# Router and experts of block one: tokens on partitions, router and experts in one stage

## What is computed

```python
expert_scores = x_flat @ router_w.T                 # 1024 x 8
top_scores, selected = jax.lax.top_k(expert_scores, 2)
top_scores = softmax(top_scores)
x1 = ragged_dot(xb, w1b, gs)                        # bf16, 64 inner units of the token's expert
x3 = ragged_dot(xb, w3b, gs)
h = silu(x1) * x3
routed = ragged_dot(h, w2b, gs)
out = sum over the two experts of routed * score
```

## Time and profile before

| | us |
|---|---|
| median of 3 runs (lowest, highest) | 1874.4 (1871.81, 1875.39) |
| the profiled execution | 1873.63 |
| its span, first to last instruction | 1871.8 |
| TensorE busy (share of the span) | 1767.7 (94%) |
| VectorE busy | 1380.0 (74%) |
| ScalarE busy | 1099.3 (59%) |
| GpSimd busy | 529.7 (28%) |
| mean granted TensorE clock, share of full | 0.959 |

### The profile page before, as it was taken

How to read it: one execution, slowest core, us unless ns; L and a number is a source line. 1 busy time by engine, 2 the same in 40 slices (tenths; PEclk the granted TensorE clock), 3 DMA queues, 4 the chain that set the end, 5 groups by cost and what they waited for, 6 DMA issues and landing times. The chain is left out here.

```text
span 1871.8 us, 29442 instructions
## 1 busy us (share of the span) xinstructions
PE 1767.7 (94%) x10475; PEld 1065.4 (57%) x10476; DVE 1380.0 (74%) x1917; ACT 1099.3 (59%) x2196; POOL 529.7 (28%) x535
## 2 busy tenths in 40 slices
PE   6999999999999999899999959999999999789997
PEld 4433333333333333644444448888888888768885
DVE  4799999999999995455999666666656666556666
ACT  2488888888887877343888625444545454234342
POOL 7346333333444402022323321111211020022223
PEclk7799999999999999968999979999999999889998
DMA  7123322223222300102546210000000000043331
GB/s 167 23 49 62 56 43 43 53 47 68 66 44 60 67 18 10 35 17 43 115 96 157 68 36 16 16 22 14 22 9 22 14 11 0 10 118 105 112 118 54
DMA packets 50606, 98.62 MB, mean 53 GB/s; under 512 B 11545, under 2 KB 21881, under 8 KB 48971
## 3 DMA queue, kind: packets, MB, share of 16 engines
q1 hardware_dynamic: 50219, 96.83, 21.9%
q10 hardware_dynamic: 288, 0.49, 0.2%
HBM read 65.63 MB, written 15.92 MB: 44 GB/s over the span
## 5 line engine op out<-in xcount | busy, mean ns | idle before, releaser
L726 DVE TENSOR_REDUCE a_max_part<-psum 128x1 f32<-128x1024 f32 x640 | 753.7, 1219 | 86.9 <-PE psum L614 85.4
L797 ACT ACTIVATE a_probs<-psum 128x512 f32<-128x512 f32 x1280 | 671.7, 601 | 184.9 <-PE psum L665 184.3
L665 PE MATMUL psum<-a_q_max,a_k_rows 51*128 51x512 f32 x1280 | 462.1, 448 | 3.4 <-ACT a_probs L797 1.8
L665 PEld LDWEIGHTS psum<-a_q_max,a_k_rows 51*128 51x128 f32 x1280 | 212.1, 186 | 353.0 <-ACT a_probs L797 285.9
L614 PE MATMUL psum<-a_k_rows,a_q_rows 48*128 48x512 f32 x1280 | 356.8, 474 | 13.8 <-DVE a_max_part L726 4.6
L654 PE MATMUL psum<-a_probs,a_v_ext 128*32 128x512 f32 x2560 | 342.5, 607 | 0.0
L614 PEld LDWEIGHTS psum<-a_k_rows,a_q_rows 48*128 48x128 f32 x1280 | 154.5, 189 | 87.7 <-DVE a_max_part L726 69.6
L1915 PE MATMUL psum<-high_t_parts,high_gu 128*128 128x512 f32 x600 | 146.2, 394 | 6.8 <-DVE high_t_parts L2009 6.8
L544 POOL TENSOR_TENSOR a_max_bf<-a_neg_max,a_zeros 128x8 bf16<-128x8 f32 x64 | 14.6, 227 | 475.0 <-issue 415.5
L417 POOL TENSOR_TENSOR a_k_rows<-a_k_in,a_k_rows 16x2048 fp32r<-16x2048 f32 x32 | 145.8, 4558 | 2.5
L1620 PE MATMUL psum<-wide_k_t,wide_q_t 128*128 128x512 f32 (+3 forms) x576 | 131.3, 355 | 1.7 <-DVE wide_id_bf L1819 1.7
(11 more groups left out here) (210 smaller groups left out, 2184.8 us busy)
## 6 DMA issues: line engine op xcount, KB each, us to landing
o<-a_o_out SPq DMA_DIRECT2D x56, 256.0 KB, 2.3
a_k_in<-in_k SPq DMA_DIRECT2D x96, 128.0 KB, 4.7
a_q_rows<-q_high SPq DMA_DIRECT2D x124, 64.0 KB, 2.4
gu_in<-in_w_gu SPq DMA_DIRECT2D x25, 256.0 KB, 2.9
high_cw<-cw SPq DMA_DIRECT2D x24, 256.0 KB, 3.9
a_v_in<-in_v SPq DMA_DIRECT2D x16, 256.0 KB, 5.8
a_o<-o SPq DMA_DIRECT2D x8, 512.0 KB, 4.4
qk_in<-in_wqk SPq DMA_DIRECT2D x16, 256.0 KB, 2.7
```

Of the source, the lines that this page charges most:

```text
L665: pe.matmul(psum[:, self.bank_of(self.filling(j)), :], k_rows[rows, b, k0:k0 + P], self.q_max[rows, u % 2, :], start=True, stop=True).then ...
L726: dve.tensor_reduce(self.max_part[:, u % 2, c // self.nch, c % self.nch:c % self.nch + 1], psum[:, 2 * (n % 2):2 * (n % 2) + 2, :], AX.XY, ...
L797: act.activation(self.probs[:, p % self.pring, :], psum[:, self.bank_of(self.filling(j)), :], ACT.Exp).then_inc(self.exp_done, 1)
```

## The change

`route` and `experts_low` of block one become one block, and the experts' part is turned round: tokens on partitions throughout.

- The chain that makes the weights moves to a helper, `router_weights`, with the same instructions; `route` stays for the second block. cw_t, the turning of e and its copy are gone for block one.
- For token tile t the stationary operand is h_bf of that tile, the moving one w1 or w3 with all 512 inner units: x1 and x3 have tokens on partitions and inner units on columns. The weight of an expert is then one number per partition for 64 neighbouring columns, and `weigh` reads e[:, t, :] broadcast, with no spread matmul.
- The weighted inner units are turned by four f32 transposes per tile (`turn`) into PSUM. ScalarE takes the high part from there (`high`), VectorE the low rest (`low`); GpSimd does nothing in this block. Both parts are double buffered by tile.
- The outputs of tile t-1 (`down`) follow the up products of tile t+2 in TensorE's order, and the gated additions are made as soon as a pair of tiles is there.
- ScalarE casts w1, w3 ahead of the Exp (whose table a dummy Exp loads), takes tiles 0 and 1 behind it, and then casts w2 (two steps), before high(0). It copies x1 and x3 both.
- TensorE does the up products of tiles 0 and 1 ahead of 50 filling matmuls in place of 70.

```diff
+            def up(t):
+                if t == 0:
+                    pe.wait_ge(w_ready, 2)
+                if t >= 2:
+                    pe.wait_ge(x1_done, t - 1)
+                    pe.wait_ge(x3_done, t - 1)
                 for i in range(2):
                     for k in range(DC):
-                        mm = pe.matmul(psum[:, 2 * (n % 2) + i, :], w_bf[:, i, k, m * P:(m + 1) * P],
-                                       h_bf[:, k, half * 512:(half + 1) * 512], start=(k == 0), stop=(k == DC - 1))
+                        mm = pe.matmul(psum[:, up_bank(t, i), :], h_bf[:, k, t * P:(t + 1) * P], w_bf[:, i, k, :],
+                                       start=(k == 0), stop=(k == DC - 1))
                 mm.then_inc(full, 1)
...
+            def turn(t):
+                pe.wait_ge(hw_done, t + 1)
+                if t >= 2:
+                    pe.wait_ge(hid_lo, t - 1)
+                for m in range(mt):
+                    mm = pe.transpose(psum[:, turned_bank(t), m * P:(m + 1) * P], hid_w[:, t % 2, m * P:(m + 1) * P], ident[:, :])
+                mm.then_inc(turned, 1)
+
+            def down(t):
+                if t == 0:
+                    pe.wait_ge(w2_ready, 2)
+                if t % 2 == 0 and t >= 4:
+                    pe.wait_ge(add_done, t // 2 - 1)
+                pe.wait_ge(hid_lo, t + 1)
                 for n in range(2 * mt):
                     m, part = n // 2, n % 2
-                    mm = pe.matmul(psum[:, 4 + t // 2, (t % 2) * D:(t % 2 + 1) * D], hid_parts[:, part, m, t * P:(t + 1) * P],
+                    mm = pe.matmul(psum[:, y_bank(t // 2), (t % 2) * D:(t % 2 + 1) * D], hid_parts[:, t % 2, part, m, :],
                                    w2[:, m, :], start=(n == 0), stop=(n == 2 * mt - 1))
                 mm.then_inc(y_full, 1)
+            keep_busy(pe, psum, ident_bf, 8)
...
+            mm.then_inc(s_full, 1)
+            up(0)
+            up(1)
+            keep_busy(pe, psum, ident_bf, 50)
+            for t in range(TT + 1):
+                if t < TT:
+                    turn(t)
+                if 2 <= t + 2 < TT:
+                    up(t + 2)
+                if t > 0:
+                    down(t - 1)
...
+            def hidden(t):
+                act.wait_ge(full, t + 1)
+                if t >= 2:
+                    act.wait_ge(hid_done, t - 1)
+                act.activation(x1[:, t % 2, :], psum[:, up_bank(t, 0), :], ACT.Copy).then_inc(x1_done, 1)
+                act.activation(x3[:, t % 2, :], psum[:, up_bank(t, 1), :], ACT.Copy).then_inc(x3_done, 1)
+                act.wait_ge(x1_done, t + 1)
+                act.activation(act1[:, t % 2, :], x1[:, t % 2, :], ACT.Silu).then_inc(silu_done, 1)
+
+            def high(t):
+                act.wait_ge(turned, t + 1)
+                if t >= 2:
+                    act.wait_ge(y_full, t - 1)
+                act.activation(hid_parts[:, t % 2, 0, :, :].rearrange("p m n -> p (m n)"), psum[:, turned_bank(t), :],
+                               ACT.Copy).then_inc(hid_hi, 1)
+
+            for i in range(2):
+                act.activation(w_bf[:, i, :, :], w_in[:, i, :, :], ACT.Copy).then_inc(w_ready, 1)
+            act.wait_ge(one_set, 1)
+            act.activation(one[:, 1:2], one[:, 0:1], ACT.Exp).then_inc(table_loaded, 1)
+            act.wait_ge(less_ready, 1)
+            act.activation(e[:, :, :], s[:, :, :], ACT.Exp).then_inc(exp_ready, 1)
+            hidden(0)
+            hidden(1)
+            act.activation(w2_bf[:, :, :], w2_in[:, :, :], ACT.Copy).then_inc(w2_ready, 1)
+            act.wait_ge(w2_ready, 1)
+            act.activation(w2[:, :, :], w2_bf[:, :, :], ACT.Copy).then_inc(w2_ready, 1)
+            for t in range(TT):
+                high(t)
+                if t + 2 < TT:
+                    hidden(t + 2)
...
+            def weigh(t):
+                dve.wait_ge(silu_done, t + 1)
+                dve.wait_ge(x3_done, t + 1)
+                dve.tensor_tensor(hid_bf[:, t % 2, :], act1[:, t % 2, :], x3[:, t % 2, :], ALU.mult).then_inc(hid_done, 1)
+                dve.wait_ge(hid_done, t + 1)
+                if t >= 2:
+                    dve.wait_ge(turned, t - 1)
+                dve.tensor_tensor(hid_w[:, t % 2, :].rearrange("p (e f) -> p e f", f=ff), hid_bf[:, t % 2, :].rearrange("p (e f) -> p e f", f=ff),
+                                  e[:, t, :].unsqueeze(2).broadcast_to([P, n_exp, ff]), ALU.mult).then_inc(hw_done, 1)
+
+            def low(t):
+                dve.wait_ge(hid_hi, t + 1)
+                dve.tensor_tensor(hid_parts[:, t % 2, 1, :, :].rearrange("p m n -> p (m n)"), psum[:, turned_bank(t), :],
+                                  hid_parts[:, t % 2, 0, :, :].rearrange("p m n -> p (m n)"), ALU.subtract).then_inc(hid_lo, 1)
...
+            for t in range(TT):
+                weigh(t)
+                if t > 0:
+                    low(t - 1)
+                if t >= 3 and t % 2 == 1:
+                    add_pair((t - 3) // 2)
+            low(TT - 1)
+            add_pair(TT // 2 - 1)
```

More of the change, by code:

```diff
@@ L1237, in route, with _ @@
         block = r.block()
[L1239 to L1244, removed]
+        @block.sync
+        def _(sp):
+            sp.wait_ge(cw_steps, 3)
+            sp.dma_start(cw_dram, cw_t[0:n_rows, :]).then_inc(stored, 16)
+            sp.wait_ge(stored, 16)
         @block.tensor
@@ L1266, in _ @@
         def _(dve):
[L1267 to L1275, removed]
-            dve.wait_ge(full, 1)
[L1277 to L1296, removed]
+            dve.memset(cw_t[:, :], 1.0).then_inc(cw_steps, 1)
+            dve.wait_ge(full, 1)
+            router_weights(dve, psum, n_exp, top, s, above, rank, best, e, total, steps, less_ready, exp_ready, cw_ready)
@@ L1312, in experts_low @@
         r = Room(nc, ctx, "low", CLEARED)
+        s = r.sb("s", [P, TT, n_exp])
+        above = r.sb("above", [P, TT, n_exp, n_exp])
+        rank = r.sb("rank", [P, TT, n_exp])
+        best = r.sb("best", [P, TT])
+        e = r.sb("e", [P, TT, n_exp])
+        total = r.sb("total", [P, TT])
+        one = r.sb("one", [P, 2])
         w_bf = r.sb("w_bf", [P, 2, DC, hid], BF16)
@@ L1328, in experts_low, with up_bank @@
+        w_ready, w2_ready, full, x1_done, x3_done, silu_done = (r.sem(n) for n in ("w_ready", "w2_ready", "full", "x1_done", "x3_done", "silu_done"))
+        hid_done, hw_done, turned, hid_hi, hid_lo = (r.sem(n) for n in ("hid_done", "hw_done", "turned", "hid_hi", "hid_lo"))
         y_full, add_done, x_done = (r.sem(n) for n in ("y_full", "add_done", "x_done"))
         block = r.block()
-        pieces = [(m, half) for half in range(2) for m in range(mt)]
+        def up_bank(t, i):
+            return 1 + 2 * (t % 2) + i
@@ L1332, in _, with turned_bank, y_bank @@
+        def turned_bank(t):
+            return 5 + t % 2
+        def y_bank(pair):
+            return (7, 0)[pair % 2]
         @block.tensor
         def _(pe):
[L1334 to L1340, removed]
@@ L1396, in _ @@
-            high(len(pieces) - 1)
-        @block.gpsimd
-        def _(pool):
-            for n, (m, half) in enumerate(pieces):
-                cut = slice(half * 512, (half + 1) * 512)
-                pool.wait_ge(hw_hi, n + 1)
-                pool.tensor_tensor(hid_parts[:, 1, m, cut], hid_w[:, m, cut], hid_parts[:, 0, m, cut], ALU.subtract).then_inc(hw_lo, 1)
+            def hidden(t):
[6 more added lines that the diff above has]
+                act.activation(act1[:, t % 2, :], x1[:, t % 2, :], ACT.Silu).then_inc(silu_done, 1)
@@ new lines, in _ @@
+            dve.memset(one[:, 0:1], 0.0).then_inc(one_set, 1)
+            dve.wait_ge(s_full, 1)
+            router_weights(dve, psum, n_exp, top, s, above, rank, best, e, total, steps, less_ready, exp_ready, cw_ready)
+            dve.wait_ge(cw_ready, 1)
+            for t in range(TT):
+                weigh(t)
[5 more added lines that the diff above has]
+            add_pair(TT // 2 - 1)
```

143 lines of the change are left out of this document (54 added, 89 removed).

## The result

The changed kernel takes 1854.0 us in the median of 6 runs (1849.7 to 1855.56), the kernel before 1873.1 on the same chip (1864.94 to 1876.77): a ratio of 0.9898, 95% interval 0.9879 to 0.9917, or 19.1 us. In a second set of runs it was 0.9899 (0.9879 to 0.992), 16.9 us between the medians. Ratios compare fast runs only; two slow executions, 2588 us of the kernel with the outputs last and 4369 us of one with early casts, are left out of them.

What follows compares the result with a forecast made beforehand. TensorE, nearly gapless at half clock, was taken to bound the old experts' stage. 44.2 us falls to 26.2, 18.0 gained, less 1.6 for a low clock: 16.4, so 1858.0 us. Range 1854 to 1865; 55% on 1856.5 to 1860.

Steps and rivals of the forecast that it cites:

- the four terms of the sum: Experts' stage after the weights: 3.2 to first turn, 5.8 to turn(2), 11.9 to turn(7), 5.3 to the end; 26.2 us.
- The gain of 18.0 without the clock's share: Experts' stage of block one: 26.2 us from weights to end in place of 44.2, before the low-clock charge.
- the hole: Sparse TensorE stretch before turn(2), ScalarE casting w2 ahead of high(0); 1.5 us of TensorE work between 794.9 and 797.8.
- The prices: Forecast step times in the new tile loop: VectorE 2.55 us a tile, TensorE 2.26 at full clock, 4.28 at half.
- Until 788.79 nothing moves: Router part ahead of the experts: same instructions, so the weights' chain ends at 788.79 us as before.
- shifts the rest by just that: Stages after the experts: whatever the changed stage gains or loses moves them by exactly that amount.
- the charge of 1.6 us for a low stretch behind the hole: New loop: two up and two down groups at clock 0.50, about half covered by waits, cost 1.6 us.
- rival 3: New loop: hole and low stretch cost nothing, TensorE recovers in the wait; 18 to 19.5 us gained, 1855 to 1856.5; 15%.
- Rival 1: New loop: clock stays at 0.50 and TensorE is the bound; gain only 8.5 us, 1866; 9%.
- The page's rule: Transposes do not count as PE-busy; the new loop would look 70% busy, not 89%, and could sink to low clock, 1866.
- Rival 2: New loop: VectorE period 0.5 longer, 3.05 us a tile, by dearer weighting or added waits; 4 us less gain, 1862; 17%.
- Rival 4: New loop: each tile passes all engines in turn, queue order making them wait; 13.5 us slower, 1888; 3%.
- the spread's 14.4 us of TensorE: Old piece loop: 16 passes of the 8-row spread matmul took 14.4 us of TensorE, listed as removed.

## Why the prediction was right, point by point

**The terms.** Against the four terms of the sum, from the completed weights: until the first turn 3.2 forecast, 3.1 measured; to turn(2) 5.8 and 5.4; to turn(7) 11.9 and 11.8; to the end 5.3 and 5.2. In all 26.2 and 25.5 (25.7 from the step's start). The gain of 18.0 without the clock's share was 18.7 measured. Of the 0.7 between them 0.4 is the hole, forecast a little too long. The prices held: up products 0.216 us each at 1.00 (the form that had been seen at 0.50 only), transposes 0.109, down 0.120, the weighting with its broadcast weight 0.692, the subtraction out of PSUM 0.684, casts 1.05. VectorE set the pitch, 5.05 a pair against 5.1.

Two sentences of the schedule hold only on average. "Until 788.79 nothing moves": the weights were complete at 791.5, 786.7 and 786.0 in the three profiles of the changed kernel and at 788.8 and 786.2 in those of the kernel before, with the router part between 3.8 and 6.2 us by the clock it got. And that the stage's gain "shifts the rest by just that" is 0.7 us too much in the two profiles with the low stretch behind the stage. Three small slips changed nothing: eight down matmuls at 0.217 are 1.74 us, not 1.71; the transposes' 17% are of the tile's 2.55 us, of TensorE's 2.26 they are 19%; and the "3.5 us of dense output matmuls" that brought the clock back had 3.6 us of up products of full height ahead of them, still at 0.50.

**The step that failed** is the charge of 1.6 us for a low stretch behind the hole. In three profiles of the changed kernel the clock is 1.00 from the first turn to the end of the loop. The hole had TensorE at work for 2.26 us of 3.5:

```profile
796.50:800.00 3.50, 2.26 (x14) 1.34 (x12) 1.79 (x4) 3.50 (x8) 0.00 (x0) 1.00 0.02 5
```

With down(0) taken out of it, in the run with the outputs last, TensorE was at work for 0.40 of 2.7 us, and there the low stretch came (one profile). The same 2.7 us, counted from turn(1), in the changed kernel:

```profile
797.20:799.90 2.70, 1.56 (x10) 1.00 (x8) 1.69 (x3) 2.70 (x7) 0.00 (x0) 1.00 0.00 0
```

The low stretch that the changed kernel does have, in two of three profiles, lies behind the stage, where the prediction had none. So rival 3, which I gave 15%, comes nearest: its gain of 18 to 19.5 us is what was measured, but not its reason. There was no low stretch from which TensorE recovered in the wait, and the hole did cost, 1.0 us of it the casts.

The time itself, 1854.0, lies at the very edge of the range, 1854 to 1865, and outside the 1856.5 to 1860 to which I gave 55%. The other two measurements of the changed kernel gave 1855.1 and, in a single execution, 1853.7: that it fell inside was partly luck. The gain of 19.1 is 2.7 above the forecast 16.4: 1.6 are this term, 0.7 the terms above, and the rest, 0.4, is within what the medians of the kernel before alone did, 1870.8 to 1874.4 from one set of runs to another; so is the difference of 1.3 in the base.

**Rival 1** (the low clock stays): refuted, by the profile and by the loop without filler, which left it within 6.8 us. **The page's rule** on transposes, from the Trainium skill, TensorE: Matmul & The Clock Gate, Part 4: PE-mode transpose, is contradicted for these f32 transposes by 5.3 us of nothing else at 1.00 (the page measured a bf16 one; no run here tests those). **Rival 2** (a longer VectorE period): not here, but its price was real: 1.66 us for the weighting as soon as GpSimd works beside it. The changed kernel escapes it since it leaves GpSimd without work. It is also what L2001's 1.193 us are made of, for which the prediction named no cause: 25 of its 50 instructions have a GpSimd step under way, and only these are slow. **Rival 4** (slower): no wait of its kind was seen; VectorE's wait in add_pair was 0.31 us at most in the loop, forecast 0.1.

**Where the 18.7 us come from.** The runs split it along one path: full-height operands bring the clock up, 3.6 (44.4 to 40.8, with some 0.5 for the extra clearing); GpSimd out of VectorE's way, 4.1 (to 36.7); the turned layout and order, 11.0 (to 25.7). Of these 4.9 are the outputs inside the loop, by the run with the outputs last (its low stretch included); some 3.7 would be the turning, copy and block end that fell away, which no run took away alone. Along another path the shares may differ. That the spread's 14.4 us of TensorE were the cost, as the prediction's list of what is removed suggests, is true only at 0.50: in the run with 128 rows and GpSimd idle the 16 passes were still there, at 1.00, and TensorE stood idle for ScalarE's copy of the weights ahead of half of the pieces, 0.2 to 1.5 us.

## What to carry to other kernels

Price a stage from the list in order of time, by starts that follow one another without a wait, and take the order in each queue seriously; four in-order queues followed gave this stage to 0.7 us. Look whether a low clock belongs to the work (operands of few rows) or to a gap, as the first lasted as long as the work here, while a dense loop left the second by itself. In a kernel whose executions spread by 6 to 12 us, read a change of one microsecond from a stretch between two events in the profile, not from medians, and ask of every other difference between two profiles whether a second profile of the same kernel repeats it.

## What the runs showed of the hardware

- VectorE's multiply with both inputs in SBUF took 1.64 to 1.66 us in place of 0.69 when a GpSimd step on SBUF (1.5 us) was under way as it started. In the kernel before, where GpSimd started 0.1 us behind it, it took 0.69 (and GpSimd's step 1.71). L2001 of the kernel before, with both inputs in f32, took 1.61 beside a GpSimd step of 1.29 that was under way, and 0.69 without. The Trainium skill, SBUF — State Buffer, section Who interferes with whom, says that such an instruction contends with a GpSimd instruction that reads SBUF; the traces agree, 1.66 against 0.69.
- The clock stayed at 0.50 through 30 us of nearly gapless matmuls, over half of their time in those of 8 rows (2.07 of 3.82 us a piece). With the same count at 128 rows it was 1.00 but for 3.4 us at the start, in spite of gaps (two profiles; in one it was at 0.50 once more, for 3.4 us, at the loop's end).
- At the head of block two's attention the clock was at 0.50 for 10 us in ten of the fourteen profiles, for 3.4 us in two and not at all in two. The three profiles of the changed kernel itself show 0, 10 and 3.4 us. Between the first two profiles that was 4.7 us of span.
